# A decoder layer on one Trainium2 core: in the expert layer VectorE copies the turned rows ahead of its register loads, and the last slot's second weights go where its first weights stood

## What is computed

```python
attn = attn @ Wo + bo
x = _layer_norm(src + attn, ln1_g, ln1_b)
keys = (x @ router_w + router_b)[..., 0]
expert_idx = jnp.remainder(jnp.floor(keys).astype(jnp.int32), N_EXPERTS)
ff_out = jnp.zeros_like(x)
for e in range(N_EXPERTS):
    h = jax.nn.relu(x @ W1[e] + b1[e])
    y = h @ W2[e] + b2[e]
    ff_out = ff_out + jnp.where((expert_idx == e)[..., None], y, 0.0)
return _layer_norm(x + ff_out, ln2_g, ln2_b)
```

## Time and profile before

| | us |
|---|---|
| median of 3 runs | 1587.26 (1586.51 to 1588.72) |
| the profiled execution | 1587.51 |
| its span on the core | 1585.6 |
| PE busy in the span | 1506.0 (95%) |
| DVE busy | 1352.6 (85%) |
| ACT busy | 1256.5 (79%) |
| POOL busy | 190.8 (12%) |

### The profile page before, as it was taken

One profiled execution on the slowest core, in us unless ns is written; L12 is line 12 of the kernel. 1 busy time (PEld: TensorE's weight loads), 2 busy tenths in 40 slices (PEclk: granted clock), 3 DMA queues, 4 the chain that ended last, 5 costly groups with the idle time before them and its releaser, 6 DMA issues.

```text
span 1585.6 us, 35391 instructions
## 1 busy us (share of the span) xinstructions
PE 1506.0 (95%) x14142; PEld 628.3 (40%) x14142; DVE 1352.6 (85%) x1914; ACT 1256.5 (79%) x2434; POOL 190.8 (12%) x236
## 2 busy tenths in 40 slices
PE   6978999999999999988999999999999999989997
PEld 6866422222222222446422222222222222338996
DVE  5765999999999999546899999999999999676654
ACT  1136589999999999767479999999999999775563
POOL 3101520000000000001560000000000000003442
PEclk9999999999999999999999999999999999999998
DMA  7000000000000000000003000000000011112111
GB/s 180 0 24 19 2 1 2 2 2 2 2 1 2 2 2 2 1 1 1 1 1 121 2 2 2 2 2 2 2 2 2 2 55 54 28 55 70 54 54 30
DMA packets 34134, 31.19 MB, mean 20 GB/s; under 512 B 10812, under 2 KB 30846, under 8 KB 33982
## 3 DMA queue, kind: packets, MB, share of 16 engines
q1 hardware_dynamic: 31246, 21.99, 5.0%
q0 software_dynamic: 2736, 7.08, 1.5%
HBM read 22.63 MB, written 6.68 MB: 18 GB/s over the span
## 4 chain that ended last, share of the span: by engine, by line
PE 71%; DVE 20%; ACT 6%; issue 3%; DMA 0%; SPq 0%; POOLq 0%; DVEq 0%; ACTq 0%
PE bank L843 24%; PE bank L830 21%; DVE nm_part L955 15%; PE s_pair L1377 4%; PE bank L1401 4%; PE s_pair L816 4%; PE s_pair L188 2%; ACT p_arena L939 2%; PE s_pair L861 1%; PE bank L627 1%; PE bank L607 1%; ACT o_sb L922 1%; PE bank L869 1%; PE bank L178 1%; PE bank L191 1%
## 5 line engine op out<-in xcount | busy, mean ns | idle before, releaser
L939 ACT ACTIVATE p_arena<-bank 128x512 f32<-128x512 f32 (+1 forms) x1856 | 1003.4, 596 | 66.7 <-PE bank L830 44.2
L955 DVE TENSOR_REDUCE nm_part<-s_pair 128x2 f32<-128x1024 f32 x896 | 1024.8, 1210 | 29.3 <-PE s_pair L816 28.1
L843 PE MATMUL bank<-p_arena,v_aug 128*32 128x256 f32 (+1 forms) x7424 | 596.0, 393 | 13.9 <-ACT o_sb L922 11.7
L816 PE MATMUL s_pair<-x_and_k,q_arena 48*128 48x512 f16 (+1 forms) x2048 | 554.0, 359 | 8.0 <-DVE nm_part L955 6.3
L830 PE MATMUL bank<-q_arena,x_and_k 49*128 49x512 f16 (+1 forms) x1856 | 550.2, 384 | 0.9 <-ACT q_arena L662 0.5
L843 PEld LDWEIGHTS bank<-p_arena,v_aug 128*32 128x32 f32 (+1 forms) x7424 | 147.4, 108 | 386.5 <-ACT p_arena L939 347.8
L830 PEld LDWEIGHTS bank<-q_arena,x_and_k 49*128 49x128 f16 (+1 forms) x1856 | 110.4, 93 | 374.2 <-ACT p_arena L939 332.3
L1031 POOL TENSOR_TENSOR attn_tok<-turned_sums,rden 128x256 f32<-128x256 f32 x30 | 18.6, 619 | 1019.6 <-DVE rden L974 1019.6
L816 PEld LDWEIGHTS s_pair<-x_and_k,q_arena 48*128 48x128 f16 x2048 | 110.6, 94 | 37.2 <-DVE nm_part L955 25.1
L1377 PE MATMUL s_pair<-q_arena 128*128 128x128 f32 x608 | 72.9, 279 | 4.3 <-issue 2.4
L1377 PEld LDWEIGHTS s_pair<-q_arena 128*128 128x128 f32 x608 | 72.2, 196 | 5.6 <-issue 2.6
(11 more groups left out here) (287 smaller groups left out, 1184.3 us busy)
## 6 DMA issues: line engine op xcount, KB each, us to landing
q_arena<-nm_T SPq DMA_DIRECT2D x512, 0.2 KB
x_and_k<-in_L_ffn_W SPq DMA_DIRECT2D x4, 1024.0 KB, 5.2
v_aug<-in_L_ffn_W SPq DMA_DIRECT2D x8, 512.0 KB, 6.0
res_rows<-x_and_k SPq DMA_DIRECT2D x1, 2048.0 KB, 8.5
x_rows<-src_sb SPq DMA_DIRECT2D x4, 512.0 KB, 3.0
x_and_k<-in_x SPq DMA_DIRECT2D x1, 1536.0 KB, 10.9
p_arena<-in_ctx SPq DMA_DIRECT2D x12, 128.0 KB, 2.0
q_arena<-in_L_attn_W_qkv SPq DMA_DIRECT2D x1, 768.0 KB, 5.5
```

The lines of the kernel that those rows point to most:

```text
L816: last = pe.matmul(m_tile[slot % 2][:, part * 512 + place:part * 512 + place + width], q_op[rows, pair, at_q:at_q + P], k_op[rows, pair, k ...
L843: last = pe.matmul(o_bank[32 * a:32 * a + 32, low:low + width], v_aug[0:m, kt, b % 4 * 4 + a, :], at.prob(4 * unit + i)[0:m, low:low + wid ...
L939: act.activation(at.prob(4 * unit + i)[0:m, :], score_bank[k % 3][0:m, :], ACT.Exp, scale=SCALE).then_inc(z["exp"], 1)
L955: dve.tensor_reduce(partials[:, first:second + 1:second - first], banks, AX.X, ALU.max, negate=True).then_inc(z["m_free"], 1)
```

## The change

`moe_vector` is changed in three places, `moe_tensor` in one. In each tick the copy of the turned rows now comes ahead of the register loads. `post_sum(1)` moves from ahead of the ticks to tick 1, behind the first copy of turned rows. And for the last slot (18) the second weights are copied in tick 20 into `last_w2`, which is the memory of `w1_use`: behind the register load and a wait for the last h matmul, and ahead of the finishing of slot 16 and of L1666 for slot 17. TensorE reads `last_w2` for the last slot.

```diff
+        last_w2 = w1_use.rearrange("p k f -> p (k f)").rearrange("p (c n) -> p c n", c=FC)
...
+                    weights = last_w2 if now == NS + 2 else w2_use
                     for c in range(FC):
-                        last = pe.matmul(bank(5 + q)[:, 0:C], hidden[:, q, c, :], w2_use[:, c, :], start=c == 0, stop=c == FC - 1)
+                        last = pe.matmul(bank(5 + q)[:, 0:C], hidden[:, q, c, :], weights[:, c, :], start=c == 0, stop=c == FC - 1)
...
+                if (i := tile_at(t, 1, NS)) is not None:
+                    dve.wait_ge(z["moe_xT_ps"], i + 1)
+                    dve.tensor_copy(xsT[:, (r - 1) % 2, :, :], bank(4 + 3 * ((r - 1) % 2))[:, 0:C].rearrange("p (k t) -> p k t", k=KC)).then_inc(z["moe_xT"], 1)
+                if now == 1:
+                    post_sum(dve, 1)
                 expert_of = {}
                 for stage in (1, 2):
                     if (i := tile_at(t, stage, NS)) is not None:
                         if not isinstance(i, int) or i >= EARLY:
                             dve.wait_ge(z["moe_late"], L_EXPERTS)
                         expert_of[stage] = dve.value_load(slot_expert[0:1, bass.ds(i, 1)], min_val=0, max_val=E - 1)
-                if (i := tile_at(t, 1, NS)) is not None:
-                    dve.wait_ge(z["moe_xT_ps"], i + 1)
-                    dve.tensor_copy(xsT[:, (r - 1) % 2, :, :], bank(4 + 3 * ((r - 1) % 2))[:, 0:C].rearrange("p (k t) -> p k t", k=KC)).then_inc(z["moe_xT"], 1)
+                if now == NS + 1:
+                    dve.wait_ge(z["moe_h_ps"], FC * NS)
+                    dve.tensor_copy(last_w2.rearrange("p c (u n) -> p (c u) n", u=2), w2_sb[:, :, bass.ds(expert_of[2] * P, P)]).then_inc(z["moe_w2"], 1)
...
-                if (i := tile_at(t, 2, NS)) is not None:
+                if (i := tile_at(t, 2, NS)) is not None and now != NS + 1:
...
             post_sum(dve, 0)
-            post_sum(dve, 1)
             moe_vector(dve)
```

## The result

| | before | after |
|---|---|---|
| median of the runs | 1587.20 us (1581.70 to 1591.22, 20 runs) | 1580.16 us (1573.65 to 1583.37, 20 runs) |
| ratio | 1 | 0.9957, 95% interval 0.9950 to 0.9964 |
| the profiled execution | 1587.51 us | 1582.69 us |
| its span | 1585.6 us | 1580.8 us |
| first gather (L1304) to the end of the span | 164.13 us | 156.24 us |

The change makes the kernel 7.0 us faster (5.7 to 7.9 us by the interval), 0.43%. The forecast was 7.9.

The account below looks back on a forecast made before the run. TensorE was taken to bound the expert layer, with gains only where it idles. Waits and clock at first h, second h and last y summed 1.80 + 1.87 - 0.12 + 4.33 = 7.88 us, giving 1579.4 us, range 1578.2 to 1582.6.

Parts of the forecast that it names:

- the three places: In the last 160 us, TensorE stands still ahead of the first h, the second h and the last y.
- Place A, wait: Ahead of the first h, the earlier copy of turned rows cuts idle time from 2.38 to 0.58 us: 1.80 us gained.
- Place A, clock: With the shorter idle time ahead, the first h takes 3.57 instead of 5.44 us: 1.87 us gained.
- Place B: TensorE's 1.9 us idle ahead of the second h keeps its length; loss of 0.12 us taken.
- the overlap: Ahead of the second h, loads wait for the copy (0.12 us loss, taken) or run beside it (0.34 us gain).
- Plain and full ticks: Loads behind the copy cost 0 in plain ticks, covered by VectorE's idle time; 0 to 0.1 us in full, taken as 0.
- 0.97 us of cover: What is left of VectorE's 2.06 us idle ahead of L1666 in plain ticks after about 1.09 us of loads.
- Place C: At the last y, 2.40 us of idle time goes and y takes 3.46 instead of 5.39 us: together 4.33 us.
- The scatter's 1.1 us of room: Slot 16's delayed scatter lands at 1570.8 us, before slot 18's add overwrites its buffer at 1571.92 us.
- The sum: 1.80 + 1.87 - 0.12 + 4.33 = 7.88 us gained, from the median of 1587.26 us to 1579.4.
- The clock rival: Half clock stays, or comes behind the second h's gap: one stretch 1581.3 us, two 1583.2; chance 0.20.
- the 0.3 us that the prediction read from a gather: Possible GpSimd cost of the moved copy of second weights, from a gather issue of 1.31 us; left out of the total.

Follow-up runs that it names:

- each profile of the end: Kernel before with only the last slot's second weights copied into the place of its first weights: 159.80 us from first gather to end, median 1583.00 us, ratio 0.9977.
- the filled gaps: Kernel before with unread matmuls in TensorE's gaps ahead of first h and last y: 9 and 10, ratio 1.0008; 4 and 5, ratio 0.9989.

## Why the prediction held, point by point

- **TensorE as the bound, and the three places.** Held. TensorE is busy 131.00 of 131.00 us again, and all the gain lies at A, B and C.
- **Place A, wait: 1.80 us forecast, 1.71 measured.** The copy could start 0.14 us behind the transposes. Its two causes were shown apart (0.87 and 0.98 us).
- **Place A, clock: 1.87 forecast.** In this pair of profiles 1.63. The size was read wrongly: 5.44 us of h was set against 3.57, a group that follows the transposes without a gap. One that starts behind a gap reads 3.81 to 3.84 at full clock, as gap B's did in the trace of before. And it is only there in part of the executions. No run showed half clock behind the 0.66 us that are left.
- **Place B: a loss of 0.12 forecast, a gain of 0.17 to 0.18 measured.** The step that failed is the overlap; I had both ends (+0.12 and -0.34 us) and took the wrong one. A load does start beside the copy. The reason given, that in the chain the sequencer's loads lie between VectorE's instructions, was read from loads that no copy stood ahead of.
- **Plain and full ticks: 0 forecast, 0 found.** The 0.97 us of cover that should be left is 1.12.
- **Place C: 4.33 forecast and 4.33 in each profile of the end against the first profile of before.** But of this 1.69 us is clock and depends on the execution; 2.64 is sure, 2.40 of wait and some 0.2 because a group without a gap ahead of it is that much shorter.
- **The scatter's 1.1 us of room** sufficed: the scatters of this stretch landed 2.1 to 2.5 us after their issue, and nothing at the end waits for a transfer.
- **The sum: 7.88 forecast, 7.04 measured by the medians.** The step that was mis-sized is the one that says "I take the slow clock to be the result of that idle time". At these places it came only behind the longer gaps: 9 of 18 from 1.96 us on, none of 16 below 1.8, the filled gaps among them. So idle time matters, but it is not sufficient, and the sum took two stretches from one profile for all executions. With the clock at full everywhere, the rest before would be 162.46 - 1.65 = 160.8 us, against 156.2 after: 4.6 us of waits. The three profiles of before have 2, 1 and 1 stretches, 1.33 on average at 1.65 us, 2.2 us. Together 6.8 us, an estimate, against 7.04 measured and an interval of 5.7 to 7.9. The profile the forecast was made from was the one with two. That 7.88 agrees with the 7.89 us between the first two profiles is partly luck: 0.09 too much for the wait at A and 0.24 for its clock stand against 0.30 too little at B.
- **The clock rival** (the first in the list, though the text on place A calls it the second) had the right mechanism for half of the difference ("part of the gain may already be in some of them") but was priced as something that happens to the changed kernel. In its two profiles the clock didn't fall at gap B. Whether the gap's 0.17 us less has to do with that (none of 4 at 1.78 to 1.79 us, 4 of 7 at 1.96) can't be settled by such counts, and a gap of 1.6 us in the attention, shown below, speaks against calling it safe.

## What to carry to other kernels

A fall of the clock behind a gap of 2 us came in some executions and not in others, so a sum made from one profile should take the wait for sure and the slow stretch by its share over several profiles. Between stages that one engine holds up, ask what stands in line ahead of the one instruction that TensorE needs; moving it ahead of register loads or statistics costs nothing as long as the engine's idle time later in the tick covers them. And where a stage writes into a single buffer, look for one that has just died at the end of the program: the last turn need not wait for the buffer that all others share.

## What the runs showed of the hardware

- The half clock behind a gap comes and goes with the execution at the same gap: 4 of 10 times behind 2.38 to 2.40 us, 4 of 7 behind 1.96. The Trainium skill (TensorE: Matmul & The Clock Gate, "HAM oscillation") warns of idle gaps longer than these; here half clock followed 9 of 18 gaps between 1.96 and 2.98 us. Such a stretch cost 1.6 to 1.7 us. The length of the gap is not all. Further up, in the attention's last part, TensorE idles for 1.55 to 1.60 us at one place in all 14 profiles. The clock was at half from the end of that gap in 6 of them, fell within 2 us in 7 more and stayed at full in one. In the first profile of before (timeline, then the stretch behind it):

```profile
1411.76 0.20 PE L1325 MATMUL s_pair<-attn_tok,band_mask 128*128 128x48 f16 x1 [1.59 <-DVE attn_tok L1482]
```

```profile
1412.50:1417.50 5.00, 5.00 (x36) 0.99 (x38) 4.76 (x25) 3.25 (x6) 0.00 (x0) 0.50 0.02 5
```

- Register loads take VectorE's time only in part when they stand behind a copy. A pair ahead of the copy of turned rows cost 1.09 us between two instructions, a pair behind it 0.84, and the chain's first piece of 0.14 us was gone.
- The first gather, behind code that is the same in all kernels of this study, was issued between 1419.64 and 1425.41 us. Effects of a few us at the end of such a program are better read from a fixed event near them than from the span.
- GpSimd's issue of a gather took 1.78 us instead of 0.97 once VectorE's copy of second weights started during it. In the changed kernel this happens to two gathers, in GpSimd's ticks 19 and 20, and so it does with the order of copy and loads alone changed:

```profile
1562.06 1.78 POOL L1310 DMA_INDIRECT x_and_k<-res_rows,attn_tok  x1 [0.30 <-issue]
...
1562.53 1.19 DVE L1686 COPY q_arena<-v_aug 128x2048 f32 x1
```

  The Trainium skill (SBUF, "SBUF: two separate sides") says that such a copy locks GpSimd out of the port while it writes descriptors. The trace agrees: the issue ended at 1563.84 us, 0.12 behind the end of the copy. With the loads twice, 14 issues that a copy started in, 0.18 to 0.55 us after their own start, all ended 0.11 or 0.12 us behind its end. So the 0.3 us that the prediction read from a gather issued in the midst of a copy were too low a price for such a case, and though the moved copy met no issue, an unmoved one did. Nobody waited for this transfer.
